# Third pass of a graph network by single messages: each tile's own wait, block additions four steps behind, odd one-hots on ScalarE

## What is computed

```python
# layer 1 (the second pass over the edges)
rst = segment_sum(h[src], dst)                     # h: normed features times a weight
rst = rst * deg_in ** -0.5 + bias
# layer 2 (the third pass)
msg = relu(x[src] + edge_attr)
h = x + segment_sum(msg, dst)
# layer 3 norms its edge input over all edges, which needs sums over the edges of
# cat(x[col], edge_attr) @ W1a and of its square:
#   per target the sum of edge_attr, and the Gram matrix edge_attr.T @ edge_attr
```

## Time and profile before

| | us |
|---|---|
| median of 3 runs | 9768.33 (9767.23 to 9770.2) |
| profiled execution, its own time | 9783.38 |
| its span from first to last instruction | 9781.0 |
| busy over the span: PE, PEld, DVE | 6958.7, 5296.4, 5640.9 |
| busy over the span: ACT, POOL | 2074.7, 6775.9 |
| second pass, first gather to last addition | 2960 to 5055 |
| third pass, first gather to last addition | 5110 to 7282 |
| mean granted TensorE clock (1 is full speed) | 0.524 |

### The profile page before, as it was taken

The page is one execution under the profiler, slowest core; times in us unless marked ns, Lnnn a source line. Parts: engine busy times, 40 slices in busy tenths (PEclk is TensorE's granted clock), DMA queues, the critical chain, the costliest instruction groups (busy, mean ns, idle before and its releaser), DMA issues. The chain is left out here.

```text
span 9781.0 us, 179091 instructions
## 1 busy us (share of the span) xinstructions
PE 6958.7 (71%) x25668; PEld 5296.4 (54%) x25669; DVE 5640.9 (58%) x22552; ACT 2074.7 (21%) x8123; POOL 6775.9 (69%) x7038
## 2 busy tenths in 40 slices
PE   2676667675768888888845555555567888888886
PEld 1555555554546666666633333333345666666664
DVE  8777777776984444444455555555554444444444
ACT  4344444443120000000002222222221222221222
POOL 0677777776737777777757777777745777777773
PEclk8555555555655555555555555555565555555556
DMA  6333333333642222222212222222212333333334
GB/s 109 96 105 105 106 105 109 103 108 94 138 93 64 55 55 55 55 55 53 57 40 54 55 53 53 53 53 53 54 23 74 80 80 82 80 82 80 82 80 34
DMA packets 625950, 724.44 MB, mean 74 GB/s; under 512 B 403289, under 2 KB 431609, under 8 KB 624766
## 3 DMA queue, kind: packets, MB, share of 16 engines
q1 hardware_dynamic: 394414, 429.07, 16.5%
q0 software_dynamic: 216064, 278.76, 12.9%
q10 hardware_dynamic: 14544, 8.74, 0.5%
HBM read 576.22 MB, written 139.85 MB: 73 GB/s over the span
## 5 line engine op out<-in xcount | busy, mean ns | idle before, releaser
L1293 POOL DMA_INDIRECT arena<-node_table,idx x3328 | 3165.0, 951 | 1091.6 <-issue 788.5
L1231 PE MATMUL banks<-arena,onehot 128*128 x7040 | 2497.3, 472 | 1245.2 <-DVE onehot L1171 608.5
L1231 PEld LDWEIGHTS banks<-arena,onehot 128*128 128x128 f32 x7040 | 1758.4, 311 | 1879.6 <-issue 1673.7
L1414 POOL DMA_INDIRECT arena<-node_table,arena x1760 | 1665.3, 946 | 552.0 <-issue 378.8
L978 POOL DMA_INDIRECT sorted_edges<-arena,idx x1664 | 1616.4, 971 | 615.7 <-issue 575.2
L1171 DVE TENSOR_SCALAR onehot<-iota_row,block_base,edge_tables 128x128 f32<-128x128 f32 x3520 | 1251.8, 357 | 608.5 <-ACTq L1277 464.1
L923 PE MATMUL banks<-arena,onehot 128*128 x3520 | 1103.9, 424 | 563.2 <-DVE onehot L872 550.3
L923 PEld LDWEIGHTS banks<-arena,onehot 128*128 128x128 f32 x3520 | 883.6, 314 | 783.2 <-issue 776.5
L1179 DVE TENSOR_TENSOR arena<-arena,banks 128x65 f32 (+1 forms) x3520 | 895.5, 254 | 583.4 <-PE banks L1231 543.7
L1390 PE MATMUL banks<-arena 128*128 128x64 f32 x3520 | 1214.1, 448 | 0.0
L1385 PE MATMUL banks<-arena 128*64 128x65 f32 x3520 | 843.0, 343 | 396.2 <-ACT arena L1401 387.5
(11 more groups left out here) (291 smaller groups left out, 6021.2 us busy)
## 6 DMA issues: line engine op xcount, KB each, us to landing
arena<-sorted_edges SPq DMA_DIRECT2D x220, 524.0 KB
arena<-in_attr_t SPq DMA_DIRECT2D x208, 512.0 KB
arena<-sorted_edges SPq DMA_DIRECT2D x110, 528.0 KB, 4.3
arena<-row_keys SPq DMA_DIRECT2D x110, 512.0 KB
arena<-in_attr_pairs SPq DMA_DIRECT2D x104, 512.0 KB
arena<-node_table,idx POOLq DMA_INDIRECT x3328, 2.4
arena<-node_table,arena POOLq DMA_INDIRECT x1760, 2.4
sorted_edges<-arena,idx POOLq DMA_INDIRECT x1664
```

Of the source, the lines that this page charges most:

```text
L1231: nc.tensor.matmul(to, m.onehot[:, j % 4, :], rows, start=True, stop=True).then_inc(s["summed"], 1)
L1293: nc.gpsimd.indirect_dma_start(slot(j), None, m.table, bass.IndirectOffsetOnAxis(ap=m.idx[:, j:j + 1], axis=0)).then_inc(gathered[j % 32], 16)
L1414: nc.gpsimd.indirect_dma_start(slots[:, j % SLOTS, 0:D], None, m.table, bass.IndirectOffsetOnAxis(ap=rec_i[:, j % SLOTS, REC_DST:REC], axis=0)
```

## The change

- **Attributes and Gram matrix change places.** The second pass now takes rows of 129 columns, gathered row, attribute and 1 (`WIDE`), in a ring of 128 tiles, so the sum of attributes per target is made there. The Gram matmul goes to the third pass, one per tile, before the step of the same index; it waits for the chunk of attributes.
- **Third pass.** The message goes to one of 8 buffers of its own (`m.messages`), made per step (1760) and no longer per tile (1664). Matmul and block addition are 64 wide. The addition runs four steps behind. VectorE makes the one-hots of even steps, ScalarE those of odd steps, as relu(1 - |column - target|), in two ACTIVATE, and per group of 8 four small ACTIVATE (128x1) that make the offsets. VectorE loads four sets of registers per group (last tile, blocks, tiles, slots), ScalarE two, TensorE none.
- **Waits of the third pass.** VectorE waits per group of 8 until the group's last tile is counted. The count is SyncE's: it waits for each gather in turn and adds one. Its loads stand between the counts: the load of the chunk that starts at tile t comes behind the count of tile t - 9. POOL waits, before every eighth gather t, for the count of tile t - 24, as in the second pass.
- **Layout.** Block rows are 130 wide (128 before); the attribute columns are cleared ahead of the second pass, not the third. The attribute copy is written with a pattern of 16 pieces of 64 floats per partition in both passes; in the second these are really apart.

The diff, cut to its core:

```diff
+WIDE = 2 * D + 1
+STEP = 2 * RW
...
+    m.second_ring = arena[:, BOTH:BOTH + RING * WIDE]
...
+    m.messages = tables[:, 1, 0:8 * D].rearrange("p (s f) -> p s f", f=D)
...
+        width, behind = {1: (WIDE, 2), 2: (D, 4)}[layer]
...
+        def load(sp, i, c):
+            t = i * RING + c * CH
+            sp.wait_ge(s["summed"], t + CH + NB - RING + SLACK)
+            settle(sp)
+            sp.dma_start(m.idx[:, c * CH:(c + 1) * CH], index[:, bass.ds(t, CH)]).then_inc(idx_in[c], 16)
...
+            sp.dma_start(to, frm).then_inc(attr_in[c], 16)
+
+        def count(engine, i, j):
+            i, j = i + j // RING, j % RING
+            if j % CH == 0:
+                engine.wait_ge(attr_in[j // CH], i * 16 + 16)
...
+            engine.wait_ge(gathered[j % 32], i * (RING // 32 * 16) + j // 32 * 16 + 16)
...
+            engine.sem_inc(s["landed"], 1)
 
         @block.sync
...
+                def rounds(i, last):
+                    for c in range(CHUNKS):
+                        if c + 1 < CHUNKS:
+                            load(sp, i, c + 1)
+                        elif not last:
+                            load(sp, i + 1, 0)
+                        for j in range(c * CH + 8, min(c * CH + CH + 8, RING) if last else c * CH + CH + 8):
+                            count(sp, i, j)
...
         @block.vector
...
+            def add_attr(base, j, slots):
+                k = base + j
+                dve.wait_ge(s["summed"], ahead(k - 8, SLACK))
+                v.tensor_tensor(m.messages[:, j % 8, :], rows[:, bass.ds(slots[j] * D, D)], attrs[:, bass.ds(slots[j] * D, D)],
+                                ALU.add).then_inc(s["sum"], 1)
...
+            def beats(base, units):
+                tiles, blocks, slots = [], [], []
+                for j in range(units + behind):
+                    if j < units:
+                        if j % 8 == 0:
+                            last = bounded_values(nc, ENG.DVE, plan[32:33, bass.ds(base + j + 7, 1)], TP - 1)[0]
                             blocks += group(nc, ENG.DVE, plan, 0, base + j, SPARE - 1)
                             tiles += group(nc, ENG.DVE, plan, 1, base + j, TP - 1)
+                            if layer == 2:
+                                slots += group(nc, ENG.DVE, plan, 2, base + j, RING - 1)
+                            dve.wait_ge(s["landed"], last + 1 + EARLY)
+                        if layer == 2:
+                            add_attr(base, j, slots)
+                        if layer == 1 or j % 2 == 0:
+                            match(base, j, tiles, blocks)
+                    if j >= behind:
+                        add_block(base, j - behind, blocks)
...
         @block.tensor
...
+                    pe.wait_ge(s["message"], k + 1)
+                    frm = m.messages[:, j % 8, :]
...
+            def add_gram(i, j):
+                if j % CH == 0:
+                    pe.wait_ge(attr_in[j // CH], i * 16 + 16)
+                attr = attrs[:, j * D:(j + 1) * D]
+                nc.tensor.matmul(m.psum[GRAM][0:D, 0:D], attr, attr, start=False, stop=False, skip_group_check=True)
+
+            with pe.Fori(0, ROUNDS) as i:
+                numbers = []
                 for j in range(RING):
+                    if layer == 2:
+                        add_gram(i, j)
+                    step(i * RING, j, numbers)
...
         @block.scalar
...
+                def aim(base, j):
+                    blocks = group(nc, ENG.Activation, plan, 0, base + j, SPARE - 1)
+                    tiles = group(nc, ENG.Activation, plan, 1, base + j, TP - 1)
+                    act.wait_ge(s["odd"], base + j + EARLY)
+                    for q in range(1, 8, 2):
+                        a_.activation(m.place[:, q:q + 1], targets[:, bass.ds(tiles[q], 1)], ACT.Identity, scale=-1.0,
+                                      bias=m.block_base[:, bass.ds(blocks[q], 1)]).then_inc(s["aimed"], 2)
+                    act.wait_ge(s["aimed"], base + j + 8)
+
+                def steps(base, units):
+                    for j in range(0, units, 2):
+                        if j % 8 == 0:
+                            aim(base, j)
+                        odd = j + 1
+                        apart = m.junk[:, odd // 2 % 2, :]
+                        a_.activation(apart, m.iota_row[:, :], ACT.Abs, bias=m.place[:, odd % 8:odd % 8 + 1]).then_inc(s["apart"], 2)
+                        relu(base + j, j)
+                        act.wait_ge(s["apart"], base + j + 2)
+                        act.wait_ge(s["summed"], base + odd - 3 + SLACK)
+                        settle(act)
+                        a_.activation(m.onehot[:, odd % 4, :], apart, ACT.Relu, scale=-1.0, bias=m.ones[:, 0:1]).then_inc(s["odd"], 2)
+                        relu(base + odd, odd)
...
         @block.gpsimd
...
-                    if layer == 1 and j % 8 == 0:
+                    if j % 8 == 0:
                         pool.wait_ge(s["landed"], i * RING + j + 8 - 32 + EARLY)
```

More of the change, by code:

```diff
@@ new lines, in _ @@
+            if layer == 1:
+                with sp.Fori(0, ROUNDS) as i:
+                    for c in range(CHUNKS):
+                        load(sp, i, c)
+            else:
+                def rounds(i, last):
+                    for c in range(CHUNKS):
+                        if c + 1 < CHUNKS:
[4 more added lines that the diff above has]
+                            count(sp, i, j)
+                sp.sem_inc(s["landed"], EARLY)
+                load(sp, 0, 0)
+                for j in range(8):
+                    count(sp, 0, j)
+                with sp.Fori(0, ROUNDS - 1) as i:
+                    rounds(i, False)
+                rounds(ROUNDS - 1, True)
@@ L1218, in _, with step @@
                                  skip_group_check=True)
[L1219 to L1221 removed]
+                pe.wait_ge(s["blank"], 1)
+            def step(base, j, numbers):
                 k = base + j
[L1223 to L1231 removed]
@@ L1250, in _ @@
-            with pe.Fori(0, ROUNDS) as i:
-                beats(i)
+                if layer == 1:
+                    if j % 8 == 0:
+                        numbers += group(nc, ENG.PE, plan, 2, k, RING - 1)
+                    frm = m.second_ring[:, bass.ds(numbers[j] * WIDE, WIDE)]
+                else:
+                    pe.wait_ge(s["message"], k + 1)
+                    frm = m.messages[:, j % 8, :]
+                if layer == 1:
+                    pe.wait_ge(s["onehot"], ahead(k, EARLY))
+                else:
+                    pe.wait_ge(s["odd" if j % 2 else "onehot"], ahead(k, EARLY))
@@ L1275, in _, with relu @@
                     for j in range(RING):
-                        act.wait_ge(gathered[j % 32], i * (RING // 32 * 16) + j // 32 * 16 + 16)
-                        act.sem_inc(s["landed"], 1)
+                        count(act, i, j)
+            else:
+                def relu(k, j):
+                    act.wait_ge(s["sum"], k + 1)
+                    row = m.messages[:, j % 8, :]
+                    a_.activation(row, row, ACT.Relu).then_inc(s["message"], 1)
+                act.sem_inc(s["odd"], EARLY)
+                def aim(base, j):
[19 more added lines that the diff above has]
+                        relu(base + odd, odd)
+                with act.Fori(0, ROUNDS) as i:
+                    steps(i * RING, RING)
+                with act.Fori(0, LAG // TAIL) as i:
+                    steps(i * TAIL + TP, TAIL)
                 act.wait_ge(s["gram_done"], 1)
```

126 lines of the change are left out of this document (34 added, 92 removed).

## The result

| | before | after |
|---|---|---|
| median of 18 runs | 9767.48 us (9763.66 to 9770.2) | 9786.72 us (9783.54 to 9788.6) |
| ratio, 95% interval | | 1.002 (1.0013 to 1.0027) |
| profiled execution | 9783.38 us, span 9781.0 | 9788.18 us, span 9786.2 |

The change costs 19.2 us. The forecast was 9779 us, 10.4 us over before, and "the same" within 0.2% (19.5 us). The measured time lies 7.7 us over the forecast and inside the range, but the difference is almost twice the forecast one and right at that bound.

What follows compares the result with a forecast made beforehand. GpSimd's gathers were taken to pace both passes, with tails behind them. Third-pass tail +14.4, cadence -5 and second pass +1 gave +10.4 us on the 9768.3 median: 9779 us, range 9755 to 9806.

Steps and rivals of the forecast that it cites:

- Release of the last places: Third pass's end: the last attribute chunk lets step 1648 start 22.5 us before the last gather starts (-24.1 to -22).
- Groups of the tail: Third pass after the last gather: 12 groups of eight steps at 7.5 us (6.8 to 8.6), 90 us in all.
- Cadence: Third pass's gathers: fewer VectorE one-hots take half of 6 ns off each, 5 us gained (nothing to 22).
- Second pass: Wider matmul and addition hide under the gathers; only its tail grows, +1 us (0 to +2).
- Rival 1: Third pass: the tail vanishes as in the second pass, 14 us instead of 79.5, 9699 us; chance 0.06.
- Rival 2: Third pass's rounds: steps cannot follow gathers, 11.2 us per group against 10.03, about 10020 us; chance 0.07.
- Rival 3: ScalarE changes tables between Abs, Relu and Identity, 1.283 us twice per odd step, 2258 us more; chance 0.02.
- Case 4: Main case but longer by over 19.5 us: tail groups of 8.3 us or more, no cadence gain; chance 0.18.

Runs made afterwards that it cites:

- the kernel with the Gram behind: Changed kernel with the third pass's Gram matmul 96 tiles behind the step: 9706.34 us on the usual-time fourth chip, 0.9928 of before.
- short loops: Changed kernel with VectorE's and ScalarE's third-pass places in loops of 32 instead of 128: 9899.79 us on the third chip, 1.0137 of before.
- with two behind: Changed kernel with the third pass's block additions two places behind instead of four: 9976.4 us on the fourth chip, 1.0205 of before.
- the kernel with the other clearing: Changed kernel with VectorE clearing 65 of the blocks' 129 columns and ScalarE 64, instead of 64 and 65: 14834 us on the second chip.

## Why the prediction was right, point by point

- **Release of the last places: right.** Forecast -22.5 us before the last gather's start. SyncE and TensorE in the changed kernel:
```profile
7161.75 0.43 SPq L1128 DMA_DIRECT2D arena<-in_attr_t  x1
```
```profile
7161.74 0.69 PE L1254 MATMUL banks<-edge_tables,onehot 128*128 128x64 f32 x2
7165.48 0.47 PE L1261 MATMUL banks<-arena 128*64 128x64 f32 x2 [3.04 <-DMA arena<-in_attr_t]
```
  The Gram matmul resumes at 7165.48, 23.3 us ahead of 7188.78; the chunk was issued 27.0 us ahead, where 27 was forecast. VectorE's first message of the tail starts at -2.3, where -1.6 was forecast. That this wait makes the tail is shown by the kernel with the Gram behind.
- **Groups of the tail: mis-sized.** Forecast 7.5 us (bounds 6.8 to 8.6), measured 7.9 to 8.2 for the first group of each loop of four and 8.5 to 8.9 for the others, 8.2 in the mean with the loop-backs and the last drain counted apart as forecast. That is 0.7 us too little, twelve times. The prediction took 1.06 us per pair; the rows have 1.26 (7248.14 to 7249.40). It took 3.0 for the gap; the rows have 3.76 (7244.13 to 7247.89). The register loads of the changed kernel on VectorE's queue (ns min/median/max), the single value in the second and in the third pass, and the sets of eight in the tail:
```profile
L1465 DVEq TENSOR_LOAD <-target_plan x218: 305/310/321, 2978.6 to 5033.1; - x109
...
L1465 DVEq TENSOR_LOAD <-target_plan x219: 529/535/547, 5127.3 to 7280.1; - x110
...
L727 DVEq TENSOR_LOAD <-target_plan x15: 602/603/824, 7245.2 to 7282.5; - x15
```
  The same load of one value takes 310 ns in the second pass, which is what the earlier trace rows gave, and 535 in the third; and one of the three sets of eight takes 824 instead of 600. These two are 0.45 of the 0.76 us. For the pairs the upper bound had named the reason, register work per message, 0.1 us each: in the changed kernel's timeline the next instruction starts 0.25 to 0.29 us after a message (7247.89 to 7248.14), where 0.14 was taken. In all, the tail came out 22 us longer instead of 14.4.
- **Cadence: right in sign, its size uncertain.** 5 us were taken, bounds 0 to 22, for half as many one-hots. The profiles give 15, or 11 with the difference between the executions taken off, and less if before is as on the first chip. The reason given does not hold: with all one-hots back on VectorE, on the first chip, the gathers did not get longer.
- **Second pass: missed.** +1 us was forecast, for its tail, which did not grow (10.1 us against 10.2); +4 to +8 came, in its gathers. 4.4 of it are the one long first gather, which no row of before announced; the rest is not explained.
- **Rival 1, no tail: rightly rejected**, for the reason given. With the Gram 96 behind it is what happens: 69.0 us below before on its chip, where 69 were worked out (9699 against 9768).
- **Rival 2, steps too slow: rightly rejected, and close.** Its threshold of 10.03 us per group holds: 8.5 to 9.0 with four behind, 10.45 with two, 10.4 in the mean of short loops, and these two come to 2.1 and 1.4% over before. The reason given against it, four pending steps cover the loads, is the one that the experiment shows.
- **Rival 3, table loads: none.** ScalarE's ACTIVATEs of the third pass take 253 to 398 ns in the mean of each line, and no table load stands among them.
- The errors offset each other, which is luck: the tail was forecast 8 us too short, the second pass 3 to 7 too short, and the cadence, by the profiles, gave back 6 to 10 us more than was taken. With 19.2 us measured, "the same" was won by a hair. Case 4, longer by over 19.5, was as near: it asked for tail groups of 8.3 us or more, which most of them were, and no gain in cadence.

## What to carry to other kernels

A planned wait is worth nothing as long as a second consumer in the same step waits in order: look for every wait of the step, and move the unplanned work (here the Gram matmul) as far back as the plan reaches. An engine's blind time between groups (register loads, a branch) must be covered by work already pending on the next engine; compare that time with the number of pending steps times their duration, here 3.5 us against 4 x 1.03 (covered) and 2 x 1.03 (not). And price a register load with its bounds check and the register work of each wait from a stretch where nothing hides them.

## What the runs showed of the hardware that was not expected

**Instructions can come late.** On two chips the kernel before took 14.4 and 14.5 ms. Single engine instructions took what they always take, GpSimd's gathers 945 ns. Register work next to VectorE's additions in the third pass (ns min/median/max), the kernel before here and then on such a chip:
```profile
L1179 DVEq FUSED_REGOPS  x1658: 57/57/65, 5114.9 to 7200.3; - x185
```
```profile
L1179 DVEq FUSED_REGOPS  x1646: 3/57/1394, 7778.3 to 10619.5; - x183
```
A stretch of it in the kernel with the other clearing, on the second of these chips:
```profile
9009.95 0.35 DVE L1186 TENSOR_SCALAR onehot<-iota_row,block_base,edge_tables 128x128 f32<-128x128 f32 x1
9011.53 0.22 DVE L1194 TENSOR_TENSOR arena<-arena,banks 128x64 f32 x1 [1.24 <-issue]
9013.71 0.23 DVE L1181 TENSOR_TENSOR edge_tables<-arena 128x64 f32 x1 [1.96 <-issue]
9017.27 0.22 DVE L1194 TENSOR_TENSOR arena<-arena,banks 128x64 f32 x1 [3.33 <-issue]
```
For 17 us the starts of VectorE's instructions lie multiples of some 0.70 us apart, as if each instruction, register work too, took that long (some 25 in all, an estimate from the gaps), once in every 16 places; in the tail it never does. That this is the fetching of instructions is argued from the steady 0.70 us, whatever the instruction, and not shown: the short loops that were to test it ran on a usual chip. On such a chip the change costs about 2% (14834 against 14532 us for the kernel with the other clearing, 1.0209, 1.0195 to 1.0223): on the first of them the third pass's gathers took 3562 us with two behind against 2854 before, while the second pass's fell from 3281 to 2902. The Trainium skill, Runtime: NRT & Kernel Launch, § Instruction fetch mechanics, says that instructions are streamed ahead and that a taken branch out of the window forces a fetch. No run here shows the second. These stretches lie in straight code, where that section expects the fetch to be mostly hidden; if they are fetches, the trace disagrees for these chips.

**The same register load has two prices in one kernel**: 310 ns for a single value in the second pass, 535 in the third, each over some 218 loads with 16 and 18 ns between the shortest and the longest. Between the passes differ what follows it in the queue (two sets of eight or three) and the registers in use; no run separates them.
